# Two stacked 3x3 convolutions with group norm: 32x32 TensorE tiles over four image quarters, one image at a time, in place of 64x64 tiles over two images

## The reference, cut to what matters

```python
x = x + conv3x3(group_norm(x), w0, padding=1) + b0
x = x + conv3x3(group_norm(x), w1, padding=1) + b1
```

## Time and profile before

| | |
|---|---|
| median of 3 runs | 4162.24 us (4153.45 to 4164.72) |
| profiled execution | span 4141.6 us from the first to the last instruction; no time of its own outside the span is shown |
| median less span | 20.6 us |
| TensorE busy | 3666.7 us, 89% of the span |
| DMA | 1435.04 MB, 346 GB/s over the span |
| mean granted TensorE clock | 0.983 of full speed |

### The profile page before, as it was taken

One profiled execution on the slowest core, in us unless ns is written; L12 is line 12 of the kernel. 1 busy time (PEld: TensorE's weight loads), 2 busy tenths in 40 slices (PEclk: granted clock), 3 DMA queues, 4 the chain that ended last, 5 costly groups with the idle time before them and its releaser, 6 DMA issues.

```text
span 4141.6 us, 88712 instructions
## 1 busy us (share of the span) xinstructions
PE 3666.7 (89%) x33232; PEld 1715.4 (41%) x33232; DVE 2025.6 (49%) x3110; ACT 1762.8 (43%) x1381; POOL 1360.0 (33%) x1829
## 2 busy tenths in 40 slices
PE   0087777898889999999888999999999999999999
PEld 0032222353334433354333443345444444566665
DVE  6866666665556344446656444444445322232222
ACT  0032222343334555543333555544443555555554
POOL 0011111121112555531111455552111455555555
PEclk9999998999999999999999999999999999999999
DMA  9989999999999999999999999999999999999997
GB/s 333 396 291 393 386 374 371 366 368 387 382 382 331 331 367 385 380 318 391 390 388 384 305 357 371 374 295 368 362 355 333 291 306 306 306 287 304 305 303 237
DMA packets 367109, 1435.04 MB, mean 346 GB/s; under 512 B 49888, under 2 KB 50016, under 8 KB 334176
## 3 DMA queue, kind: packets, MB, share of 16 engines
q10 hardware_dynamic: 176736, 627.30, 47.9%
q0 software_dynamic: 153344, 536.96, 34.5%
q1 hardware_dynamic: 36864, 268.45, 16.9%
HBM read 895.64 MB, written 536.87 MB: 346 GB/s over the span
## 4 chain that ended last, share of the span: by engine, by line
PE 56%; DMA 15%; ACTq 11%; issue 10%; DVE 5%; ACT 2%; DVEq 0%; POOL 0%; POOLq 0%; SPq 0%
PE conv L653 56%; DMA out_dram<-out_tile 12%; ACTq L479 11%; DMA stat_tile<-x_dram 2%; DVE bn_x L700 2%; ACT out_tile L465 1%; DVE bn_mid L710 1%; DMA mid_dram<-out_tile 1%; DVE out_tile L727 1%; DVE mv_mid L738 1%; DVEq L700 0%; DVE mv_x L732 0%; PE conv L555 0%; ACTq L461 0%; PE conv L583 0%
## 5 line engine op out<-in xcount | busy, mean ns | idle before, releaser
L653 PE MATMUL conv<-x_tile,wts 64*64 64x512 f32 x32832 | 3648.7, 598 | 235.5 <-ACT out_tile L465 140.4
L653 PEld LDWEIGHTS conv<-x_tile,wts 64*64 64x64 f32 x32832 | 1694.9, 134 | 2170.3 <-issue 2037.0
L465 ACT ACTIVATE out_tile<-conv,bias 128x1024 f32<-128x1024 f32 x688 | 728.6, 1110 | 1340.5 <-PE conv L653 791.1
L710 DVE BATCH_NORM_STATS2 bn_mid<-out_tile 128x512 f32 (+1 forms) x1376 | 849.3, 680 | 881.1 <-ACT out_tile L465 880.9
L727 DVE TENSOR_SCALAR out_tile<-conv,bias 128x1024 f32<-128x1024 f32 x340 | 436.4, 1284 | 1168.7 <-PE conv L653 856.7
L371 POOL DMA_DIRECT2D mid_dram<-out_tile x680 | 343.4, 507 | 1708.1 <-ACT out_tile L465 1641.4
L470 ACT ACTIVATE out_tile<-conv,bias 128x1024 f32<-128x1024 f32 x344 | 383.1, 1114 | 764.4 <-PE conv L653 505.6
L508 ACT ACTIVATE x_tile<-x_tile 16x2048 f32<-16x2048 f32 x340 | 648.6, 1908 | 44.9 <-issue 31.6
L700 DVE BATCH_NORM_STATS2 bn_x<-stat_tile 128x512 f32 (+1 forms) x1024 | 628.7, 678 | 45.6 <-DMA stat_tile<-x_dram 45.5
L405 POOL COPY x_tile<-x_tile 16x2048 f32<-16x2048 f32 x340 | 639.1, 1880 | 1.7
L385 POOL DMA_DIRECT2D out_dram<-out_tile x680 | 348.3, 514 | 823.7 <-DVE out_tile L727 758.8
(11 more groups left out here) (62 smaller groups left out, 114.5 us busy)
## 6 DMA issues: line engine op xcount, KB each, us to landing
x_tile<-x_dram ACTq DMA_DIRECT2D x680, 512.0 KB, 23.0
stat_tile<-x_dram SPq DMA_DIRECT2D x256, 1024.0 KB, 9.8
out_dram<-out_tile POOLq DMA_DIRECT2D x680, 384.0 KB, 7.8
mid_dram<-out_tile POOLq DMA_DIRECT2D x672, 384.0 KB, 9.3
x_tile<-mid_dram ACTq DMA_DIRECT2D x340, 640.0 KB, 6.4
x_tile<-mid_dram ACTq DMA_DIRECT2D x344, 128.0 KB, 8.5
mid_dram<-out_tile POOLq DMA_DIRECT2D x8, 416.0 KB, 10.0
x_tile<-x_dram ACTq DMA_DIRECT2D x8, 256.0 KB
```

Of the source, the lines that this page charges most:

```text
L465: last = act.activation(out_tile[0:parts, slot, i], conv[0:parts, bank, i], ACT.Identity, bias=bias0[0:parts, win.parity, int(unit.last), ...
L653: last = nc.tensor.matmul(to, weights, x_tile[HALF * half:HALF * (half + 1), slot, middle, c + kw:c + kw + BANK], start=(kw == 0), stop=(k ...
L710: last = dve.bn_stats(bn_mid[0:parts, unit.win.pair % 2, i, bass.ds(unit.n * 2 + h, 1), :] .rearrange("p a b -> p (a b)"), out_tile[0:part ...
```

## The change

The kernel's body is written anew; the launch is the same. What it does:

- **Quarters.** Each image is cut into four quarters of 256 rows. Partitions 32q to 32q + 31 hold 4 rows x 8 channels of quarter q, a block. `x_tile` has 4 slots of four blocks (16 rows of each quarter). A unit is 16 rows of each of the four quarters, 64 rows; an image has 16 units a layer, and 8 images x 2 layers x 16 = 256 units in all.
- **Matmuls of 32x32.** Output block j of quarter q comes from input block j (weights `MAIN`) and from the next one (`NEXT`), each with three `kw`: 2 halves x 2 x 3 x 4 blocks x 4 quarters = 192 calls a unit (49152 in all; 16416 before). The quarter is the row tile and a PSUM bank, the block is the column tile. The last block of a quarter takes its `NEXT` from `tail_tile`. PSUM is two halves of four banks, one for each half of the columns.
- **One image at a time.** Layer 0 of image n, then layer 1 of image n, then the next image. Layer 0's statistics of image n + 1 are made during image n, but layer 1's only after the last unit of layer 0 (`sums_of` at the end of `window`): TensorE waits there.
- **No overlap is read.** Layer 0 reads x once for the matmuls (and once for the statistics), without the 8/6; the halo copies are gone. Each quarter has an edge (the block before its first row) and a tail (the block after its last).
- **Queues.** GpSimd issues x's loads, 16 of 128 KB a unit (one a block and quarter), and the out stores, 4 of 512 KB a unit. SP issues the statistics' loads, the mid stores (4 of 512 KB a unit) and the mid loads (4 of 512 KB a unit). ACT issues none and makes all evictions: two of 128x2048 a unit. DVE evicts nothing.
- **Layer 1's columns** are row by channel in a block, so a quarter's 128 partitions of `out_tile` are 16 rows x 8 channels and leave in one transfer.
- The loops over images are written out for the first and the last image, with a hardware loop for the six between; units are written out.

```diff
-ROWS_IN = 8
-ROWS_OUT = 6
-BANDS = 2
-X_RING = 8
-WINDOWS = (Window(0, 0, 0, 1, 8, 0), Window(1, 0, 1, 2, 4, 0), Window(2, 1, 0, 2, 4, STATS // 2),
...
+QUARTERS = 4
+TILE = P // QUARTERS
+BLOCKS = 4
+BLOCK_ROWS = 4
+X_RING = 4
+RING = 4
...
+    conv = ctx.enter_context(nc.psum_tensor("conv", [P, HALVES, QUARTERS, BANK], F32))
...
+        def _(sp):
+            def store_mid(win, u):
+                slot = u % RING
+                sp.wait_ge(evicted, HALVES * (win.g + u + 1))
+                for q in range(QUARTERS):
+                    row = CH * (QUARTER * q + UNIT_ROWS * u)
+                    sp.dma_start(mid[bass.ds(win.n, 1), row:row + P, :].rearrange("n a w -> (n a) w"),
+                                 out_tile[:, slot, q]).then_inc(stored[0][slot], 16)
+            def load_mid(win, u):
+                first = 0 if u else 1
+                for q in range(QUARTERS):
+                    row = QUARTER * q + UNIT_ROWS * u + BLOCK_ROWS * first - 1
+                    sp.dma_start(x_tile[TILE * q:TILE * (q + 1), u % X_RING, first:BLOCKS, 1:SIDE + 1],
+                                 mid_rows(win, row, BLOCKS - first)).then_inc(rows_loaded[1][u % X_RING], 16)
+            def image(n):
+                win, after = Window(0, n), Window(1, n)
+                for u in range(UNITS):
+                    stats_of_next(win, u)
+                    store_mid(win, u)
+                    first = u - (UNITS - X_RING)
+                    if first >= 0:
+                        sp.wait_ge(stored[0][first % RING], stores_through(win, first))
+                        load_mid(after, first)
+                for s in range(RING):
+                    sp.wait_ge(stored[0][s], stores_through(win, UNITS - RING + s))
+                load_edge(after)
+                for u in range(UNITS):
+                    stats_of_next(after, u)
+                    if u + X_RING < UNITS:
+                        sp.wait_ge(conv_done, HALVES * (after.g + u + 1))
+                        load_mid(after, u + X_RING)
+                    if u == 0:
+                        load_tail(after)
...
+        def _(pool):
+            def store_out(win, u):
+                pool.wait_ge(evicted, HALVES * (win.g + u + 1))
+                for q in range(QUARTERS):
+                    row = QUARTER * q + UNIT_ROWS * u
+                    pool.dma_start(out[bass.ds(win.n, 1), :, row:row + UNIT_ROWS, :]
+                                   .rearrange("n c r w -> (n r) c w"),
+                                   out_tile[:, slot, q]).then_inc(stored[1][slot], 16)
+            def load_x(n, u):
+                for j in range(BLOCKS):
+                    for q in range(QUARTERS):
+                        row = QUARTER * q + UNIT_ROWS * u + BLOCK_ROWS * j - 1
+                        if row >= 0:
+                            pool.dma_start(x_tile[TILE * q:TILE * (q + 1), u % X_RING, j, 1:SIDE + 1],
+                                           x_block(n, row)).then_inc(rows_loaded[0][u % X_RING], 16)
+            def image(n):
+                for u in range(UNITS):
+                    pool.wait_ge(conv_done, HALVES * (win.g + u + 1))
+                    if u + X_RING < UNITS:
+                        load_x(n, u + X_RING)
...
+                for u in range(UNITS):
+                    store_out(after, u)
+                    if not after.last_image and u >= UNITS - X_RING:
+                        load_x(n + 1, u - (UNITS - X_RING))
+                        if u == UNITS - 2:
+                            pool.wait_ge(pad_known, after.w + 2)
+                            load_edge(n + 1)
...
+        def _(act):
+            def evict(win, u, c):
+                act.wait_ge(conv_done, HALVES * (win.g + u) + (c + 1))
+                if c == 0 and (u >= RING or win.before(RING)):
+                    act.wait_ge(stored[earlier.layer][slot], stores_through(earlier, (u - RING) % UNITS))
+                act.activation(out_tile[:, slot, :, c * BANK:(c + 1) * BANK], conv[:, c],
+                               ACT.Identity, bias=bias[:, win.layer:win.layer + 1]) \
+                   .then_inc(evicted, 1)
...
+        def _(pe):
+            def convolve(win, u):
+                for c in range(HALVES):
+                    wait_for_bank(win, u, c)
+                    for part in (MAIN, NEXT):
+                        for kw in range(KW):
+                            at = c * BANK + kw
+                            for j in range(BLOCKS):
+                                here = u * BLOCKS + j + part
+                                for q in range(QUARTERS):
+                                    rows = slice(TILE * q, TILE * (q + 1))
+                                    last = nc.tensor.matmul(
+                                        conv[TILE * j:TILE * (j + 1), c, q],
+                                        wts[rows, win.layer, part, kw], moving,
+                                        start=(part == MAIN and kw == 0),
+                                        stop=(part == NEXT and kw == KW - 1))
+                    last.then_inc(conv_done, 1)
...
+        def _(dve):
+            def window(win):
+                for u in range(UNITS):
+                    if win.layer == 0:
+                        take_mid(win, u, 0)
+                    if not win.last_image:
+                        for i in (STATS_1 if win.layer else STATS_0)[u]:
+                            take_x(win.n + 1, i, i // STAT_SLOTS + 1)
+                    if win.layer == 0:
+                        take_mid(win, u, 1)
+                    if win.layer == 1 and u == SUM_MEAN and not win.last_image:
+                        sums_of(win.w + 1, 0)
+                if win.layer == 0:
+                    dve.wait_ge(mid_taken, HALVES * UNITS * (win.n + 1))
+                    sums_of(win.w + 1, 1)
```

More of the change, by code:

```diff
@@ L411, in _ @@
[L411 to L430 removed]
+                    ident[part, 0, MAIN, 0:3 * CH].rearrange("p (t c) -> p t c", c=CH),
@@ L949, in _taps @@
+            sums_of(0, 0)
+            assert steps[0] == AT_START
+            images(dve, window)
 def _taps(weight, np):
```

1071 lines of the change are left out of this document (393 added, 678 removed).

## The result

The changed kernel is slower. Its median is 5323.73 us (5311.07 to 5333.33, four runs), the kernel before ran in 4159.84 us beside it (four runs): a ratio of 1.2815, 95% interval 1.2778 to 1.2853. The profiled run took 5311.07 us with a span of 5309.6 us. I had forecast 3800 us and a range that ended at 4450.

The account below looks back on a forecast made before the run. TensorE bounded the last windows, DMA the first layer-0 stretches; afterwards mostly DMA. Start 130 + layers 0 1504 + waits 440 + layers 1 1390 + waits 294 + end 22 = 3780 us, plus 20.6, gave 3800 us; range 3600 to 4450.

Parts of the forecast that it names:

- The step that failed: Instruction fetches with all units written out: up to 17 MB, 1% of the bytes, left to the range.
- TensorE's term: Matmuls in every unit: a set of 16 tiles costs 0.43 us, a unit 10.3 us, 256 units 2640 us.
- TensorE's rival: Every unit: TensorE can't keep 16 tiles busy; time 296 + 256u, 4370 us or 5570 us at eight tiles; chance 0.28.
- under "wrong": Signs in the profile: layer gaps as short as 17 us, DMA far below 370 GB/s, units over 15 us.
- bursts without overlap: Case of TensorE's rival: bursts of 16 follow each other, 0.66 us a set, 15.9 us a unit, 4370 us.
- DMA's rate: The 16 DMA engines give 378 GB/s on this mix; a middle image's layer 0 takes 193 us, layer 1 175.
- stages 1 and 3: Layer 0 and layer 1 of each image, first matmul to last: summed over the images, 1504 and 1390 us.
- the drains: Waits between layers, narrow loads slowed by 1.4: 55 us x 8 ahead of layer 1, 42 x 7 ahead of layer 0.
- the Trainium skill's rule: Partitions 0 to 31 and 32 to 63 reach the same ports; loads of quarters 0 and 1 get half rate: 3960.
- the sums: Between layer 0 and layer 1: eviction, statistics, aggregation and chain, some 17 us, covered by SP's 46 us of transfers.
- GpSimd's rival: GpSimd's queue of x's loads becomes the bound, deciding from 1.0 us an issue; 4300 us at 1.25 us; chance 0.07.
- The start: Before the first matmul: one image's statistics and x, 42 MB in 118 us, then sums; TensorE starts at 130 us.

Follow-up runs that it names:

- the control: The changed kernel with a constant tile as the matmuls' moving operand, all transfers and waits kept: 5316.68 us.
- the looped kernel: Against the control, TensorE's units 1 to 14 of layer 0 and 1 to 11 of layer 1 put in a hardware loop: 4595.57 us.
- an eighth of the columns: The control, still written out, with transfers of x, mid and out moving 128 of 1024 columns and statistics loads of 256 KB for 1 MB: 3588.77 us.
- two queues: The looped kernel with x's loads ordered 0, 2, 1, 3, plus mid loads split: SP issues quarters 0 and 1, ACT 2 and 3: 4198.13 us.

## Why the prediction was wrong

**The step that failed** is the one on instruction fetches: all units written out "need up to 17 MB, 1% of the bytes. I leave that to the range." The bytes were right (12.89 MB, 1.0% of the engines' time). I priced them as bytes and not as something that TensorE waits for. The rate at which it asks was in my own numbers: 256 instructions at 32 a set are 8 sets, 8 x 0.43 = 3.4 us for a block of code, where the kernel before has 13.8 us. From the control to the looped kernel 721 us go with the fetches. That is a lower bound of what late code costs in the changed kernel: 220 us of such stops are left in the looped one, and it pays for the wait for pads besides. The control against an eighth of the columns, 1728 us, is an upper bound, since it takes the transfers' own limits away too. Of these 1728 us, 1109 are idle time ahead of the matmuls and 576 are matmuls that run longer, at the lower clock.

**TensorE's term.** "If 16 tiles run as four do, a set costs 0.43 us": it's 0.52 us, so the unit is 12.4 us, not 10.3, a loss of 2.1 x 256 = 540 us of TensorE's time. Eight tiles of 32x32 do run at 0.43 us a set, so what I carried over from four tiles holds for eight and fails at sixteen. With DMA as the bound most of it would have been hidden, as the forecast said (up to 13 us a unit). It matters where a unit is behind: the layers of the written-out kernel with an eighth of the columns take 200 and 207 us in the mean, above my 193 and 175 us of DMA.

**TensorE's rival** has the formula that comes nearest and the wrong reason. The mean unit took (2443 + 2453) / 256 = 19.1 us, and 296 + 256 x 19.1 is 5190 us, within 2.5% of 5311; the page shows what I wrote under "wrong": waits of 26 and 8 us between layers and DMA far below 370 GB/s. But sets of 16 do overlap, 0.52 us a set where one after the other would take 0.66; it stood for code. So the rival's nearness in time is luck. My range ended at bursts without overlap, 15.9 us a unit. The Trainium skill's 10.6-fold for 16 tiles (TensorE: Matmul & The Clock Gate, "Measured speedup vs the span model") gave 0.65 us a set; the stream here runs at 0.52, so the measurement speaks against carrying that figure to a stream.

**DMA's rate.** 378 GB/s was the right price for the mix and the wrong one for this order of loads. It is passed in the middle of layer 0, at 386 GB/s, once quarters 0 and 2 alternate, with 348 over the layer; with 0, 1, 2, 3 it is 338 in the same place and 315 over the layer. "In stages 1 and 3 loads mix with stores on another queue, and the 376 GB/s of rows 3 hold with such narrow loads": those of layer 1 went to 80 partitions over both halves and to 16, those of layer 0 to all 128, these to 32 of one half. The loss of rate that I allowed only in the drains was in the layers: 189 us by the order of x's loads, most of it in layer 0, and 208 us by two queues for mid's, in layer 1. The 3960 us that I gave for the Trainium skill's rule put it in the drains alone as well.

**The drains.** Forecast 55 and 42 us; measured 26 and 8 in the changed kernel, 29 and 20 in the looped one, 28 and 22 with two queues. At 270 to 277 GB/s the drain is slow, as said. But few bytes are left for it: after the last matmul of the second image's layer 0 (1087.9 us) SP issues only the last unit's stores, one unit's loads and the edge, where I had put the stores and loads of four units. And the sums are not covered, as I had them: of the eight waits ahead of layer 1 in the changed kernel four end with the edge's loads, as forecast, and four with the sums, which came late behind a statistics tile. Where the transfers are narrow, the sums alone take 17.5 us, as forecast. The 20 and 22 us ahead of layer 0 in the looped kernels are mostly the wait for the fourth slot's pads.

**The rest.** GpSimd's rival falls: 0.550 us an issue, 1082 us of 5310, with 1053 us of idle time before them. The start was 135 us for 130, the end 18 for 22. ACT's eviction is 1967 ns for 128x2048, 3.9 us a unit for 4.4. All of these were within a few us.

**Together.** 5317 us, less 721 for the loop, 189 for the order and 208 for two queues, is 4198 us, by single runs on three chips, whose kernel before ran in 4159 to 4174 us. So with most of the code on the chip and the loads spread the new tiling comes level with the old one, and the smaller reads of x have not yet bought anything. No version with all the transfers beats the kernel before. What is left in the last one are 56 units of code outside of the loops and waits between layers of 222 and 152 us. Of the 152 some 90 come from the looped edit's wait for pads (57 us in the changed kernel); without it the time would be some 4100 us, an estimate that no run bears out. Nor was a looped version run that computes the reference's result with `x_tile`. Whether late fetches stand behind other packets in the engines' queues or behind them in memory stays open as well; the runs only show that they come late with the load.

## What to carry to other kernels

Before a loop is written out for smaller matmuls, divide: 256 instructions of TensorE are one fetch of 16 KB, and if they last 4 us while the DMA engines are full, TensorE stands waiting for code (at 13.8 us it didn't, and at 6.9 us hardly, though it also waited for data there); keep such a body in a loop (99 KB stayed on the chip). A step down in tile size multiplies instructions: price them by time per block of code, not by their bytes. Order loads to 32 partitions so that those in flight together reach different halves of the partitions; a second queue for them helped here too, though perhaps for the same reason. And when an experiment moves a wait, look whether the new wait costs something by itself.

## What the runs showed of the hardware that I had not expected

- Idle time called "issue" in steady bursts of 128 records is late code: 348 stops of 3.55 us in the median, half of them ending 1.34 to 1.51 us after a fetch of 1.1 us.
- The same 787 fetches cost 1094 us of "issue" at 256 GB/s, 268 us at 153 GB/s and too little to be listed at 60 GB/s.
- 16 tiles of 32x32 run at 32.4 ns a record, 0.52 us a set, in either order of the tiles; eight at 0.43 us a set, and four of 64x64 at 0.43.
- The stops also cost clock. From 160 to 200 us the granted clock was 0.97, and 128 records took 4.45 us; from 600.29 to 607.11 us, from the last part of an idle time of 4.6 us on, it was 0.50, the level of 1.2 GHz, and the first 128 records took 6.92 us. Over the span the mean granted clock is 0.883, against 0.983 in the kernel before:

```profile
600.29:607.11 6.82, 5.40 (x99) 2.62 (x100) 0.00 (x0) 0.00 (x0) 0.00 (x0) 0.50 1.02 353
```

```profile
601.71 6.92 PE L531 MATMUL conv<-x_tile,wts 32*32 32x512 f32 x128 [4.61 <-issue]
609.02 8.69 PE L531 MATMUL conv<-x_tile,wts 32*32 32x512 f32 x255 [0.39 <-issue]
```
